# A three-layer recommender kernel on one core: layer 1 spread between the transposes, layers 2 and 3 of the block before one step at a time

## What is computed

```python
e = emb_tables[jnp.arange(F)[None, :], x]          # B=1024, F=32, D=64
gram = jnp.einsum('bid,bjd->bij', e, e)
iu, ju = jnp.triu_indices(F, k=1)
cross = gram[:, iu, ju]
h = jnp.concatenate([e.reshape(B, F * D), cross], axis=1)
h = jax.nn.relu(h @ W1 + b1)                       # 1024 wide
h = jax.nn.relu(h @ W2 + b2)                       # 512 wide
logits = h @ W3 + b3                               # 1000 wide
return jax.nn.sigmoid(logits)
```

## Time and profile before

| what | value |
|---|---|
| three timed runs | 486.14, 490.38, 490.88 us (median 490.38) |
| profiled execution | 488.51 us, span of the core 486.7 us |
| PE busy | 383.4 us (79%), 3840 matmuls |
| POOL busy | 313.9 us (64%), nothing after slice 33 of 40 |
| DVE, ACT busy | 260.4 us (53%), 209.6 us (43%) |
| DMA | 80.24 MB, mean 165 GB/s |
| granted TensorE clock | 0.93 of full speed on average |

### The profile page before, as it was taken

The page is one execution under the profiler, slowest core; times in us unless marked ns, Lnnn a source line. Parts: engine busy times, 40 slices in busy tenths (PEclk is TensorE's granted clock), DMA queues, the critical chain, the costliest instruction groups (busy, mean ns, idle before and its releaser), DMA issues.

```text
span 486.7 us, 9671 instructions
## 1 busy us (share of the span) xinstructions
PE 383.4 (79%) x3840; PEld 377.5 (78%) x3840; DVE 260.4 (53%) x630; ACT 209.6 (43%) x326; POOL 313.9 (64%) x517
## 2 busy tenths in 40 slices
PE   0066666479798764899999976899999959999895
PEld 0066666379797764889999976889999949999895
DVE  3133333253688342365569863645788745564750
ACT  3022222142574231454457553544486525543542
POOL 6788887887888877777877877777778730000000
PEclk9998787889899787799999997999999979999999
DMA  7323343317746433249966652679667625795512
GB/s 241 113 60 101 106 111 111 116 33 239 238 149 190 113 107 109 60 157 319 287 214 176 210 184 64 187 241 318 183 174 235 190 96 172 260 281 175 155 36 84
DMA packets 32606, 80.24 MB, mean 165 GB/s; under 512 B 6802, under 2 KB 13106, under 8 KB 32050
## 3 DMA queue, kind: packets, MB, share of 16 engines
q1 hardware_dynamic: 24370, 71.22, 45.6%
q0 software_dynamic: 8192, 8.40, 7.8%
HBM read 69.22 MB, written 10.39 MB: 164 GB/s over the span
## 4 chain that ended last, share of the span: by engine, by line
POOL 50%; PE 33%; issue 13%; DMA 1%; DVE 1%; ACT 0%; ACTq 0%; POOLq 0%; DVEq 0%
POOL emb L287 41%; POOL gap L293 10%; PE h1p L467 6%; PE h1p L469 6%; PE h1p L468 6%; PE misc L467 4%; PE misc L469 4%; PE misc L468 4%; PE misc L499 2%; PE misc L482 1%; DMA emb<-tables_dram,idx 1%; DVE dg L413 1%; DMA xi<-x_dram 0%; DVE h2lo L429 0%; ACT h2f L348 0%
## 5 line engine op out<-in xcount | busy, mean ns | idle before, releaser
L287 POOL DMA_INDIRECT emb<-tables_dram,idx x256 | 255.8, 999 | 77.2 <-POOL gap L293 74.7
L396 DVE TENSOR_TENSOR wlo<-wraw,whi 128x256 fp32r<-128x256 f32 (+1 forms) x448 | 159.0, 420 | 66.7 <-ACT whi L310 65.7
L467 PE MATMUL h1p<-xhi,whi 128*128 128x256 f32 x512 | 151.9, 297 | 1.0 <-ACT h1f L339 1.0
L468 PE MATMUL h1p<-xlo,whi 128*128 128x256 f32 x512 | 149.8, 293 | 0.0
L469 PE MATMUL h1p<-xhi,wlo 128*128 128x256 f32 x512 | 149.4, 292 | 0.0
L310 ACT CAST whi<-wraw 128x1024 fp32r<-128x1024 f32 (+1 forms) x112 | 117.4, 1049 | 72.2 <-PE h1p L469 41.8
L467 PEld LDWEIGHTS h1p<-xhi,whi 128*128 128x128 f32 x512 | 103.6, 202 | 3.3 <-issue 3.1
L468 PEld LDWEIGHTS h1p<-xlo,whi 128*128 128x128 f32 x512 | 103.1, 201 | 0.0
L469 PEld LDWEIGHTS h1p<-xhi,wlo 128*128 128x128 f32 x512 | 102.8, 201 | 0.0
L482 PE MATMUL misc<-ident,emb 128*128 128x128 f32 x128 | 26.4, 343 | 84.4 <-DMA emb<-tables_dram,idx 84.4
L482 PEld LDWEIGHTS misc<-ident,emb 128*128 128x128 f32 x128 | 18.3, 174 | 87.4 <-DMA emb<-tables_dram,idx 69.8
(11 more groups left out here) (34 smaller groups left out, 466.8 us busy)
## 6 DMA issues: line engine op xcount, KB each, us to landing
wraw<-w_dram SPq DMA_DIRECT2D x96, 512.0 KB, 4.4
wraw<-w_dram SPq DMA_DIRECT2D x16, 500.0 KB, 3.6
emb<-tables_dram,idx POOLq DMA_INDIRECT x256, 3.0
gram_scratch<-dg SPq DMA_DIRECT2D x4, 1024.0 KB, 5.0
out_dram<-res SPq DMA_DIRECT2D x16, 250.0 KB
gram_scratch<-dg SPq DMA_DIRECT2D x4, 512.0 KB, 6.7
gc<-gram_scratch SPq DMA_DIRECT2D x16, 128.0 KB, 5.1
xi<-x_dram SPq DMA_DIRECT2D x1, 128.0 KB, 2.1
```

The lines of the kernel that those rows point to most:

```text
L287: nc.gpsimd.indirect_dma_start(emb[:, n % 2, k, t, f * D:(f + 1) * D], None, tables, bass.IndirectOffsetOnAxis(ap=idx[:, BT * n + t, 2 * k ...
L396: last = nc.vector.tensor_tensor(wlo[:, u % RING, part], wraw[:, u % RAWS, part], whi[:, u % RING, part].bitcast(fp32), ALU.subtract)
L467: nc.tensor.matmul(dst, whi[:, slot, cols], hi, start=start, stop=False, skip_group_check=True)
L468: nc.tensor.matmul(dst, whi[:, slot, cols], lo, start=False, stop=False, skip_group_check=True)
```

## The change

The list of items is made anew. In blocks 1 to 3 a new function `steps_with_previous` lays a fixed round behind the transposes of pair m: one step of layer 2 or 3 of the block before, and the two emb steps of pair m-1. Behind the last transposes stand l3 2 and emb 12 alone, then gram. Of layer 1, emb 13, 14 and 15 are kept for the time between gram and the pair steps. The transposes of pairs 0 and 1 of block n+1 no longer stand between the pair steps of block n but behind all four of them and l3 n-1 3, next to each other. Block 0 follows the same pattern without the steps of a block before. The two conditions on `s_dga` and `s_dgv` in layers 2 and 3, which guard PSUM banks that gram uses, count the grams that stand ahead in the list. No instruction is added or taken away; every step, cast and DMA of the block is there as often as before.

```diff
+    def steps_with_previous(n):
+        yield ("tr", n, 1)
+        yield from emb(n, 0, 2)
+        yield from l2(n - 1, 0)
+        for m in range(2, KP):
+            yield ("tr", n, m)
+            yield from (l2(n - 1, m - 1) if m <= 4 else l3(n - 1, m - 5))
+            yield from emb(n, 2 * m - 2, 2 * m if m < KP - 1 else 2 * m - 1)
...
-            for k in range(4):
-                yield from emb(n, k, k + 1)
-                yield ("tr", n, k + 2)
-                yield from l2(n - 1, k)
-            yield from emb(n, 4, 5)
-            yield ("tr", n, 6)
-            yield from emb(n, 5, 6)
-            yield ("tr", n, 7)
-            yield from l3(n - 1, 0)
-            yield from l3(n - 1, 1)
-            yield from emb(n, 6, 8)
+            yield from steps_with_previous(n)
         yield ("gram", n)
-            yield from emb(n, 8, 11)
+        yield from emb(n, 13, 15)
         yield ("move", n)
-            yield from l3(n - 1, 2)
-            yield from emb(n, 11, 14)
+        yield from emb(n, 15, 16)
         yield ("pairs", n)
-        yield from emb(n, 14, 16)
         yield ("pair", n, 0)
-        if n + 1 < BLOCKS:
-            yield ("tr", n + 1, 0)
         yield ("pair", n, 1)
         yield ("pair", n, 2)
-        if n + 1 < BLOCKS:
-            yield ("tr", n + 1, 1)
         yield ("pair", n, 3)
         yield ("h1", n)
         if n > 0:
             yield from l3(n - 1, 3)
+        if n + 1 < BLOCKS:
+            yield ("tr", n + 1, 0)
```

More of the change, by code:

```diff
@@ L44, in l3 @@
         yield ("out", n, k)
+    def steps_with_previous(n):
[6 more added lines that the diff above has]
+            yield from emb(n, 2 * m - 2, 2 * m if m < KP - 1 else 2 * m - 1)
     yield ("tr", 0, 0)
-    yield ("tr", 0, 1)
     for n in range(BLOCKS):
         if n == 0:
-            for m in range(2, KP - 1):
-                yield from emb(n, 2 * m - 4, 2 * m - 2)
+            for m in range(1, KP - 2):
+                yield from emb(n, 2 * m - 2, 2 * m)
                 yield ("tr", n, m)
             yield from emb(n, 10, 11)
-            yield ("tr", n, KP - 1)
+            yield ("tr", n, 6)
             yield from emb(n, 11, 12)
-        else:
-            for k in range(4):
-                yield from emb(n, k, k + 1)
-                yield ("tr", n, k + 2)
-                yield from l2(n - 1, k)
-            yield from emb(n, 4, 5)
-            yield ("tr", n, 6)
-            yield from emb(n, 5, 6)
-            yield ("tr", n, 7)
-            yield from l3(n - 1, 0)
-            yield from l3(n - 1, 1)
-            yield from emb(n, 6, 8)
-        yield ("gram", n)
-        if n == 0:
+            yield ("tr", n, 7)
             yield from emb(n, 12, 13)
         else:
-            yield from emb(n, 8, 11)
+            yield from steps_with_previous(n)
+        yield ("gram", n)
+        yield from emb(n, 13, 15)
         yield ("move", n)
-        if n > 0:
-            yield from l3(n - 1, 2)
-            yield from emb(n, 11, 14)
-        else:
-            yield from emb(n, 13, 14)
+        yield from emb(n, 15, 16)
         yield ("pairs", n)
-        yield from emb(n, 14, 16)
         yield ("pair", n, 0)
-        if n + 1 < BLOCKS:
-            yield ("tr", n + 1, 0)
         yield ("pair", n, 1)
         yield ("pair", n, 2)
-        if n + 1 < BLOCKS:
-            yield ("tr", n + 1, 1)
         yield ("pair", n, 3)
@@ L111, in used_after, with grams_before @@
         return STEP[item] + 1
+    def grams_before(*item):
+        return sum(o[0] == "gram" for o in ITEMS[:ITEMS.index(item)])
     def outs_before(item):
@@ L522, in layer2 @@
                         pe.wait_ge(s_sig, 4 * n)
-                    grams = GROUPS * (n + 1)
-                    pe.wait_ge(s_dga, grams)
-                    pe.wait_ge(s_dgv, grams)
+                    pe.wait_ge(s_dga, GROUPS * grams_before("l2", n, k))
+                    pe.wait_ge(s_dgv, GROUPS * grams_before("l2", n, k))
                 for c in range(4):
@@ L540, in layer3 @@
                     pe.wait_ge(s_sig, 4 * n + k - 1)
-                    if n + 1 < BLOCKS:
-                        pe.wait_ge(s_dga, GROUPS * (n + 2))
-                        pe.wait_ge(s_dgv, GROUPS * (n + 2))
+                    pe.wait_ge(s_dga, GROUPS * grams_before("l3", n, k))
+                    pe.wait_ge(s_dgv, GROUPS * grams_before("l3", n, k))
                 for c in range(H2 // P):
```

## The result

The changed kernel takes 498.7 us (496.6 to 500.39) where the kernel before takes 489.7 us (486.14 to 490.88): the ratio is 1.0185, with a 95% interval of 1.0148 to 1.0222. It is 1.85% slower, and the interval leaves out "no change". The forecast was 489.4 us with a range up to 498.0 and "no change" as the likeliest case. The rival that ends slower, a long round trip, was nearest in time.

The account below looks back on a forecast made before the run. Gathers bound the kernel up to 395.99 us, then PE's tail; the tail loses 14.7 us, PE arrives 13.7 later through round trips, clock and borders, so 1.0 us less: 489.4 us, range 479 to 498.

Parts of the forecast that it names:

- a long round trip: Rival: dot products' write and reads land among weight loads, trips reach 20.2 us, time 500.4 us, +2.1%; chance 0.25.
- The bound before: Kernel before: gathers set the blocks' times up to 395.99 us, PE's slack is small, then 90.7 us of PE work.
- The cover before: Steps between gram and pair 0 before the change: four in block 0, nine (26 us) in blocks 1 to 3.
- The tail is eight steps shorter and its gain is paid for on the way: Behind the last transposes: 18 steps instead of 26; tail loses 14.7 us, PE arrives 13.7 us later.
- PE is behind the gathers for good: From block 1's pair 7 (200.1 us) on: PE needs 104.8 us a block against 99.6 for the gathers.
- The round trip: From gram's end to pair 0: 16.5 us in blocks 1 to 3, three steps covering 8.7, new wait 7.8 us.
- The estimate of 12.9 us: Round trip by the skill's fit: write 5.6 us, read 3.2; three trips 10.8 us less than in the sum.
- The clock: Low clock behind each new PE wait costs 1.57 us; four pair steps take 13.09 us.
- The border: Between blocks: emb 0 starts at P + 7.6, or P + 6.2 between blocks 0 and 1; PE waits 4.0 us.
- P: The time at which a block's four pair steps end.
- The signs: Expected in the profile: gclo waits 6 to 10 us, border waits about 4, pair 7 of block 3 at 405 to 413.
- PE keeps pace: Rival: PE reaches pair 7 of block 3 at 395.99; span 473.6, time 477.3 us, -2.7%; chance 0.12.

Follow-up runs that it names:

- g2: Kernel before with only the next block's first two transposes moved behind all pair steps and l3 3: 488.23 us, ratio 0.9997.
- g1: Changed kernel with the reads of the dot products one step earlier, so one weight load instead of two follows the write: 489.53 us, ratio 1.0011.
- g4: Changed kernel measured once more, unaltered, on the first kind of chip: 498.9 us, ratio 1.0185 to the kernel before.
- g3: Changed kernel with six emb steps behind gram, transposes back between pair steps, l3 2 ahead of pair 7's transposes: 472.93 us, 0.9712 of the kernel before.
- e4: Changed kernel with 60 unused matmuls ahead of each gclo wait and 28 ahead of each border wait: 487.72 us, 0.9973 of the kernel before.
- e1: Changed kernel with six emb steps instead of three behind gram in blocks 1 to 3: 475.26 us, 0.971 of the kernel before.
- e3: Changed kernel with six emb steps behind gram in blocks 1 to 3 and transposes back between the pair steps: 475.86 us, 0.967 of the kernel before.
- f4: Kernel before, unchanged, profiled on the second kind of chip: 520.35 us.
- f3: The kernel of g3 on the second kind of chip: 534.58 us, 1.0267 of the kernel before there.
- e9: Kernel before without POOL's filler instruction and its wait between gathers, on the second kind of chip: 664.71 us.

## Why the prediction was wrong, point by point

- *The bound before* was right: the gathers up to 396, and PE's slack small. g2 measured that slack by filling it.
- *The cover before* was counted rightly in the prediction, four steps in block 0 and nine in the others; "three to seven" emb steps in the description of the kernel should read four in block 0 and eight, with l3 2 beside them, in the others.
- *The tail is eight steps shorter and its gain is paid for on the way* was right in kind. Forecast: pair 7 of block 3 at 409.7 and a tail of 76.0. Measured: 419.66 and 78.7. "PE is behind the gathers for good" held from block 1 on (204.30, forecast 200.1).
- *The round trip*, the step "I take 16.5, near block 0", was mis-sized. From gram's end to pair 0 it was 18.2, 19.5, 16.6 and 17.0 us, for 16.0 (block 0) and 16.5, together 5.7 us more. The text saw the second weight load between write and reads and gave it half a microsecond; g1 against g4 shows that it is worth 1.4 to 3.7 us a trip. Block 0, from which the size was taken, had only one load there, and the sum left its own trip at 15.97 although it has two with the change. The estimate of 12.9 us from the fit of the Trainium skill ("DMA: Bandwidth & Descriptors", "Anatomy of one DMA") was further off on the same side: even g1's trips with one load are 14.9 to 15.9. The Trainium skill gives that fit for DMAs issued by gpsimd, and these are issued by SP beside other loads, so the miss says nothing against it in its own place.
- *The clock*, 1.57 us behind each wait, was mis-sized too. The price came from one wait of 4.20 us. Most waits cost more: four pair steps took 14.23, 12.91, 14.24 and 13.97 us for 13.09, the first two emb steps 8.35, 8.50 and 7.32 for 7.33, and the last four l2 steps 13.08 for 11.58, although the wait of 2 us ahead of them is the same as before. Together 6.7 us over the forecast. The price is 1.4 to 2.7 us a wait and does not grow with the wait: the longest, 10.56 us, cost the least, and two border waits of 4.00 us cost 2.7 and 1.6. What sets it stays open. g1, g3 and g4 have the l2 steps at 13.06, 11.58 and 11.58, so that last term comes and goes. e4 confirms the mechanism: with PE kept busy in the waits the clock stays at 1.00 and the extra time is gone.
- *The border*, P + 7.6 and P + 6.2, was 7.9 twice and 6.5: right.
- The differences sum to 5.7 + 6.7 + 0.9 = 13.3, against 12.7 of span (498.4 for 485.7). The forecast, 1.0 us less, lay 5.9 us under "over 1% slower"; the clock's 6.7 us alone use that up, the trip's 5.7 almost. Both were sizes taken from block 0 of the kernel before, and both were too small.
- *A long round trip* came nearest in time (500.4), but by luck for about half of it: it needed trips of 20.2 us in blocks 1 to 3, and they were 17.7 on average. By the trips alone the change would have stayed under 1% slower.
- *The signs.* The waits for `gclo` (7.7 to 10.6 us for 6 to 10) and at the borders (5.5, 4.0, 4.0 for about 4) and the transposes without a wait came as forecast. Pair 7 of block 3 (419.66 for 405 to 413), the tail (78.7 for 76) and the last gather (at 387.6 for 394) did not. PE's waits put down to `wlo` are those of the border, not a late weight.
- *PE keeps pace* was wrong for the changed kernel, and its condition and its time (473.6 of span) are what e1 and e3 reached once the round trip was covered.

## What to carry to other kernels

Steps that are moved ahead are taken from the wait that they used to cover. Before a list is made shorter at its end, count what still stands between a write to DRAM and the use of what is read back, and keep that much. A stall on an engine is free only as long as the same engine waits for something later in the same period; past that point each one is paid in full, with the low clock behind it on top, as here. A price taken from one block's trace should be taken with the transfers that stood around it.

## What was not expected of the hardware

- On one kind of chip a stream of small matmuls ran at a fifth of its speed while gathers were in flight (gram 26.1 to 31.2 us in f4 against 5.6), with idle time that no semaphore explains; on the other it did not. The order of steps that gains 2.9% on the first kind (g3) took 2.7% longer there (f3, interval -1.2 to 6.6%), so at least the gain is not shown there. The cause is open. Blocks of instructions that arrive late do not fit the slow stretch of e9, in which none moved; how else gathers and PE get in each other's way, no run separates.
- On that kind of chip a filler of 0.23 us with its wait between the gathers is worth over 140 us: 664.71 us without it against 522.82 with it.
- A second 512 KB load, issued about 4 us ahead of four 128 KB reads, went with a landing of 4.7 instead of 3.2 us (block 0 of g4 and g1), and with round trips longer by 1.4 to 3.7 us.
- The same wait of 2.0 us ahead of the last layer 2 steps was followed by a lower clock in some profiles (13.08 us for four steps) and not in others (11.58).
